# Moving the stage of x behind the projection, and the x loads among the weight transposes, in a linear attention and gated FFN kernel

## The reference

```
xn  = layernorm(x)
q, k, v = xn @ wq.T, xn @ wk.T, xn @ wv.T          # 16 heads of 64
qf, kf  = elu(q) + 1, elu(k) + 1
kv      = sum over rows of kf^T v                  # per head 64 x 64
attn    = (qf @ kv) / (qf . sum over rows of kf + 1e-6)
r   = sigmoid((mu_r*xn + (1-mu_r)*xn_prev) @ W_r.T)
ffn = r * (relu((mu_k*xn + (1-mu_k)*xn_prev) @ W_k.T)^2 @ W_v.T)
y   = x + attn @ wo.T + bo + ffn
```

## Time and profile before

| | |
|---|---|
| median of 3 runs | 2350.32 us |
| the profiled execution | 2352.19 us |
| its span, slowest core (core 0) | 2350.7 us |
| spans of the 8 cores | 2336.7 to 2350.7 us |
| TensorE busy | 1881.6 us (80%) |
| VectorE busy | 1477.3 us (63%) |
| ScalarE busy | 570.0 us (24%) |
| first and last exponential of the first pass (L363) | at 195.6 and 768.5 us |
| mean granted TensorE clock | 0.929 of full |

### The profile page before, as it was taken

How to read it: one execution, slowest core, us unless ns; L and a number is a source line. 1 busy time by engine, 2 the same in 40 slices (tenths; PEclk the granted TensorE clock), 3 DMA queues, 4 the chain that set the end, 5 groups by cost and what they waited for, 6 DMA issues and landing times.

```text
span 2350.7 us, 27068 instructions; the slowest of 8 cores (2336.7 to 2350.7 us)
## 1 busy us (share of the span) xinstructions
PE 1881.6 (80%) x9092; PEld 821.8 (35%) x9092; DVE 1477.3 (63%) x2235; ACT 570.0 (24%) x1026; POOL 461.3 (20%) x395
## 2 busy tenths in 40 slices
PE   0007988889999498988979889798898988978978
PEld 0003444444444133333323333243332333323333
DVE  0005666676666666858668586685775866858664
ACT  0004444444443122021221211212212122021220
POOL 0000101111011012303223132140321412304123
PEclk9999999999999789989989899898998989989988
DMA  9983558523231212112112021121211212112011
GB/s 108 108 125 99 109 135 161 111 88 93 79 99 55 63 31 62 61 30 90 37 55 72 22 87 36 55 72 37 73 47 44 73 36 73 54 37 72 31 41 63
DMA packets 112522, 165.88 MB, mean 71 GB/s; under 512 B 66865, under 2 KB 83249, under 8 KB 111938
## 3 DMA queue, kind: packets, MB, share of 16 engines
q0 software_dynamic: 25136, 98.58, 16.7%
q1 hardware_dynamic: 87250, 65.57, 12.0%
HBM read 113.78 MB, written 65.01 MB: 76 GB/s over the span
## 4 chain that ended last, share of the span: by engine, by line
PE 41%; DVE 25%; issue 14%; ACT 9%; SPq 6%; DMA 3%; POOL 1%; DVEq 1%; ACTq 0%; POOLq 0%
PE B L580 11%; PE B L642 7%; PE B L653 6%; SPq L202 6%; PE B L664 5%; PE B L340 4%; DVE diffT L508 4%; PE B L350 4%; DVE aT L553 3%; ACT eT L556 3%; DVE rb L616 3%; DVE xk L517 2%; DVE aT L360 2%; ACT xn_tm L249 2%; ACT xn_tm L246 2%
## 5 line engine op out<-in xcount | busy, mean ns | idle before, releaser
L545 PE MATMUL B<-XF,WT_wq 128*128 128x512 bf16 x1024 | 254.9, 411 | 95.8 <-DVE qm L559 80.1
L702 POOL TENSOR_TENSOR tt<-tt,x 128x1024 f32<-128x1024 f32 x64 | 165.7, 2589 | 828.4 <-DVE tt L688 821.6
L340 PE MATMUL B<-WT_wk,XF 128*128 128x512 bf16 x1024 | 245.7, 383 | 51.4 <-DVE kf_tm L367 51.4
L642 PE MATMUL B<-WT_wr,xr 128*128 128x512 bf16 x1024 | 266.8, 408 | 0.0
L580 PE MATMUL B<-xk,WT_wkf 128*128 128x512 bf16 x1024 | 252.9, 413 | 0.2
L653 PE MATMUL B<-WT_wvf,k_act 128*128 128x512 bf16 x1024 | 249.1, 387 | 0.0
L671 ACT ACTIVATE poolr<-B 128x512 f32<-128x512 f32 x128 | 76.4, 597 | 706.7 <-PE B L642 660.6
L350 PE MATMUL B<-WT_wv,XF 128*128 128x512 bf16 x1024 | 242.7, 380 | 0.0
L664 PE MATMUL B<-WT_wo,qm 128*128 128x512 bf16 x1024 | 241.9, 379 | 0.0
L513 DVE SCALAR_TENSOR_TENSOR xr<-diffT,mur_sb,XF 128x512 bf16<-128x512 f32 x128 | 208.0, 1625 | 13.9 <-DVE diffT L508 0.5
L698 POOL TENSOR_TENSOR x<-x,bo_bc 128x1024 f32<-128x1024 f32 x64 | 150.5, 2351 | 311.7 <-DMA x<-x 264.5
(11 more groups left out here) (70 smaller groups left out, 2088.0 us busy)
## 6 DMA issues: line engine op xcount, KB each, us to landing
x_tm<-x SPq DMA_DIRECT2D x64, 512.0 KB, 3.8
x<-x POOLq DMA_DIRECT2D x64, 512.0 KB, 5.3
y<-tt POOLq DMA_DIRECT2D x64, 512.0 KB, 3.2
xnt<-XF POOLq DMA_DIRECT2D x128, 128.0 KB, 4.2
XF<-xnt SPq DMA_DIRECT2D x112, 132.0 KB, 3.3
wbf_wk<-wk POOLq DMA_DIRECT2D x1, 2048.0 KB, 23.9
wbf_wv<-wv POOLq DMA_DIRECT2D x1, 2048.0 KB, 43.4
wbf_wq<-wq POOLq DMA_DIRECT2D x1, 2048.0 KB, 61.3
```

The lines of the kernel that those rows point to most:

```text
L340: ev = E("pe", lambda e, q=q, c=c, g_in=g_in, h=h, kb=kb: e.matmul(PS[kb][:, :], XF[q][:, c, 16 + 128 * g_in:16 + 128 * g_in + 128], WT["w ...
L545: e.matmul(PS[bank][:, :], WT["wq"][:, c, dc * 128:(dc + 1) * 128], XF[q][:, c, 16:528], start=(c == 0), stop=(c == NCH - 1)),
L642: b_r=b_r: e.matmul(PS[b_r][:, :], xr[q][:, c, g_in * 128:(g_in + 1) * 128], WT["wr"][:, c, h * 512:(h + 1) * 512], start=(c == 0), stop=( ...
L702: ev_t4 = E("gps", lambda e, pa=pa: e.tensor_tensor(tt3[pa], tt3[pa], x2, ALU.add), waits=[h_t3[(ga, 0)], h_t3[(ga, 1)]], inc="gps", fwait ...
```

## The change

Two things are changed. First, the transposes of wk and wv are no longer issued ahead of all loads of x. They are spread over the stages of the first four groups: behind the x load of each of them stand four transposes, two of wk and two of wv. Second, in the main loop the stage of the group one tile ahead is called behind `p1_proj` of the current group, not in front of it.

```
-    emit_wtp("wk", "dWTa", ev_cast2)
-    ev_wTa = emit_wtp("wv", "dWTa", ev_cast2)
+    ev_wTa = None
...
     for g_in in range(GPT):
         do_stage(0, g_in)
+        for nm in ("wk", "wv"):
+            for c in (2 * g_in, 2 * g_in + 1):
+                ev_wTa = E("sync", lambda e, nm=nm, c=c: e.dma_start(
+                    WT[nm][:, c, 0:1024], wbf_h[nm][:, c * 128:(c + 1) * 128],
+                    transpose=True),
+                    waits=[ev_cast2] if (g_in == 0 and nm == "wk" and c == 0)
+                    else (), inc=("dWTa", 16))
...
                 evabs[gg + 1] = t_group(tj % 2, (gg + 1) % GPT, gg + 1)
-            if ti + 1 < ntiles:
-                do_stage(ti + 1, g_in)
             evAB = evabs.pop(gg)
             evac4 = evAB[1]
             p1_proj(q, evAB, g_in, gg)
+            if ti + 1 < ntiles:
+                do_stage(ti + 1, g_in)
```

## The result

The changed kernel takes 2381.06 us (median), the kernel before 2350.29 us in the same runs. The ratio is 1.0143, with a 95% interval of 1.0116 to 1.0169: slower by 1.4%, or 34 us (the medians differ by 31). I had forecast 2387 and slower. All ratios here leave out executions in which one die ran at a lower clock; the medians do not. The profiled execution of the changed kernel has a span of 2377.1 us (core 2), against 2350.7 (core 0). Over all eight cores the last wv matmul of the first pass (L350, now L349) starts at 764.5 to 772.4 us before and at 795.2 to 800.2 after, so the pass ends 31 us later on average. What follows is as long as before: 1574 us on average from there to the end of the span before, 1573 after.

A forecast was written before the change was run, and what follows sets the result against it. The prediction took a closed chain through VectorE and ScalarE to bound the first pass. From 2352.2 us, plus 48.4 for the longer period, minus 12 at the start, came 2388.6, given as 2387 for the median; range 2370 to 2404.

The forecast's parts named there:

- What bounds the pass, and its period: First pass: a closed chain through VectorE and ScalarE holds it; uncovered XF copies lengthen its period from 8.89 to 9.75 us.
- The count of periods: First pass: 58 periods of 9.75 us plus 12.2 of irregular delays put group 61 48.4 us later.
- The start: Before the first pass: weight transposes spread among x loads bring the first L340 from 191.1 to 179, gain 12 us.
- A: First pass: longer TensorE idle gaps lower its clock in half of the groups, 2435 us in all; chance 0.05.
- B: First pass: TensorE is freed, the 51.4 us of kf_tm waits go, period 8.0, 2287 us; chance 0.03.
- C: First pass: XF copies keep a cover, period stays 8.89, only the earlier first matmul counts, 2338 us; chance 0.06.

The follow-up runs named there:

- the second edit alone: Kernel before with only the stage moved behind the projection, all 16 transposes still ahead of x; ratio 1.0192, 45 us more.
- the third experiment: Changed kernel with t_group called two groups ahead, so the XF copies stand behind the projection and in front of the stage; ratio 0.9924.
- the kernel with the exponentials hidden: Kernel before with transposes spread among x loads, stage in front, and VectorE's order aT0, v0, aT1, kf0, kf1, v1; ratio 0.9735.

## Why the prediction was right

**What bounds the pass, and its period: right.** 9.75 was forecast, 9.75 measured. The wait at st_mean was to be about 1.0 and is. TensorE's wait was to go to about 100 us and came out lower: 93.9 on core 2, where each wait holds the 0.22 us of the unrecorded matmul, and 79.8 to 86.5 on the six cores whose longest is 1.64. That the copies, not the stage, are the price is shown by the kernel with the copies in front (8.90) and by the pair without the row sum (8.67 both).

**The count of periods: right, a little high.** TensorE's timeline of groups 3 and 61; both rows miss their first matmul, so both starts lie 0.22 earlier:

```profile
201.71 1.67 PE L339 MATMUL B<-WT_wk,XF 128*128 128x512 bf16 x7 [1.30 <-DVE kf_tm L366]
...
777.48 1.67 PE L339 MATMUL B<-WT_wk,XF 128*128 128x512 bf16 x7 [1.73 <-DVE kf_tm L366]
```

From 175.59 to 777.26 are 601.7 us, where I had 604.0. Over the eight cores the stretch from the first wk matmul to the end of the last wv matmul has grown by 47.8 us on average, where I had 48.4. The start of group 3 was forecast at +26.3 and came at +25.9. Between groups 3 and 61 are 575.8 us, 10.3 over 58 periods of 9.75; I had kept 12.2. What Square waited for in the pass, the counterpart of the earlier trace rows:

```profile
  DMA x_tm<-x: 1.5, 1
```

On core 2 it was 2.3 us before and is 1.5 now; on average over the cores 4.1 have become 0.9, so the slower pass did give the loads time, as argued. What makes the rest of the difference stays open.

**The start: right in kind, mis-sized.** I took 12 us. It was 15.5 from core 0 before to core 2 after, and 16.6 on average over the eight cores (14.3 to 18.7). The term was three x tiles at 184 GB/s, 8.5 us, put on top of 170.1, for the last transpose to land at 178.6. Both parts were too large. The last transpose landed at 167.2 before and at 173.7 after (averages; 174.5 on core 2), so the three tiles put it off by 6.5 us. And 170.1 was the landing of x tile 0, 2.9 us behind the last transpose. I had this tile "change places with an equal piece", but in the changed kernel it had landed at 124.0, while the casts still ran, and cost nothing at the end. One rate does not fit this stretch either: on core 2 the engines moved 171 GB/s at a busy share of 1.06 from 160 to 165, and 245 at 1.01 from 165 to 170.

What is late last is not the transposes but, just behind them, the fourth stage: x tile 3 is issued at 163.56, Square starts at 168.82, the first copy stands behind that stage's normalisation at 173.69, and TensorE's second group of transposes waits for the copies until 174.78. On the eight cores the last weight transpose had landed 0.4 to 1.7 us before the first wk matmul. The averages add up: 4.6 us here (16.6 less 12) and 0.6 in the pass make 5.2, and the pass ends 31.2 us later on average where I had 36.4. The profiled execution was forecast at 2388.6 and took 2378.7; the other 4.7 us of that difference lie between single cores and executions.

**The rivals.** A (the clock) did not come as a price in every group: the granted clock is 1.00 from 600 to 760 in the rows above, and from 200 to 790 it is 0.98 to 0.99 on the eight cores, against 0.97 to 0.98 before. But I had taken the gap of 1.5 us for the harmless one, and in some groups the clock fell all the same. In the changed kernel no gap of TensorE in the pass is over 1.9 us except one of 6.1 at the extraction, and still the clock of core 2 fell to half four times, for 3.4 to 6.8 us. The first of them, and L339 in it, 3.00 us where it takes 1.67 elsewhere:

```profile
280.60:284.00 3.40, 3.40 (x9) 0.50 1.22 249
```

```profile
280.43 3.00 PE L339 MATMUL B<-WT_wk,XF 128*128 128x512 bf16 x7 [1.72 <-DVE kf_tm L366]
```

On the eight cores it was at half clock for 10 to 24 us of the pass, as in the kernel before. The section on HAM oscillation in the Trainium skill's "TensorE: Matmul & The Clock Gate" warns of gaps between bursts; here 56 groups have the gap and only a few the half clock, and no run shows what sets those apart.

B and C would have shown a period of 8.0 or 8.9; it is 9.75, in the changed kernel and with the second edit alone. C's premise, that the copies might keep a cover, is what the third experiment builds on purpose.

## What to carry to other kernels

Before an instruction is moved in an in-order queue, look at what lies in the shadow of another engine's answer there: an instruction can be free only because of where it stands. Two neighbours swapped on one engine put 0.86 us on a closed chain here, in each of some 60 groups, with every engine's busy time unchanged. And sum the chain against the engine that should be the bound, for its slack decides what an exposed piece costs: 0.86, 0.24 or 0.00 a group in three kernels with the same swap.

## What the runs showed of the hardware

**A small transfer can wait for large ones, packet by packet.** The first x tile, 0.5 MB, was issued by SyncE at 3.29 us and landed at 124.0, while seven casts of 2 MB went through GpSimd's queue. Of the small constants (4 to 32 KB, issued before it) the last was there at 84.4. The Trainium skill, "DMA: Bandwidth & Descriptors", in the section on queues, rings and completion order, says that each DMA engine takes turns between its queues by packets. The trace agrees. Core 2 of the changed kernel from 84 to 124 us, with q0 GpSimd's queue and q1 SyncE's (packets, MB, share):

```profile
DMA packets 320, 4.72 MB, mean 118 GB/s; under 512 B 64, under 2 KB 64, under 8 KB 192
...
q0 software_dynamic: 160, 4.19, 93.4%
q1 hardware_dynamic: 160, 0.53, 6.0%
```

The turns are even, 160 to 160, and they were 162 to 162 from 45 to 84. The packets are not: 128 of those of the casts hold 4.19 MB, 32 KB each, and 128 of those of SyncE's queue are the tile, 4 KB each. So on each of the 16 engines the tile needs eight turns, and each turn goes by with a large packet of a cast, some 4 us. A small transfer in many small packets fares no better: muk_sb is 4 KB, one packet of 32 bytes for each of its 128 rows, and from 52 to 84 us the two queues have 144 packets each. The weight transposes, issued from 45 on, wait in the same way until the casts are through; in the kernel before the two queues also have 160 packets each from 84 to 124. With five of the casts gone from the start, the tile landed at 47.

**A clock of 0.81 on two cores at a time.** In the kernel with the exponentials hidden (ratio 0.9735), TensorE's rows of core 0 and of core 2 (us, busy, clock, DMA share, GB/s):

```profile
220.00:240.00 20.00, 20.00 (x117) 0.81 0.33 106
```

```profile
220.00:240.00 20.00, 19.89 (x148) 1.00 0.43 132
```

Cores 0 and 1 had 0.81 of the full clock from 200 to 380 us, and eight matmuls took 2.27 us instead of 1.89; their first pass ended at 726 and 729 us, that of the six other cores at 698 to 712. In the second profile of the same kernel no core showed it. It does not need a full first pass: the kernel with the copies in front had it too, on cores 6 and 7, from 930 to 990 us, in the second pass, which no edit touches. The Trainium skill, "TensorE: Matmul & The Clock Gate", in the section "Seeing it yourself", describes a limiter that takes a whole die to 13/16 (0.81) of the clock when three or more of its cores run dense matmuls. The level agrees; that two cores of the die had it while the other two had 0.99 in the same time (0.96 and 0.97 in the second case) does not. What sets it off no run here shows.
